# Second attention of a two-layer block: keys and values projected as four row groups of 32, and a new order of a step

## The reference, cut to what matters

```python
def _L1_xattn_ref(x, cond, w_q, w_k, w_v, w_out, b_out):     # x layer-normed, cond = ctx_768
    q = (x @ w_q).reshape(B, SQ, 16, 64)
    k = (cond @ w_k).reshape(B, SKV, 16, 64)                  # 96 -> 1024
    v = (cond @ w_v).reshape(B, SKV, 16, 64)                  # 96 -> 1024
    attn = softmax(einsum('bqhd,bkhd->bhqk', q, k) * 64 ** -0.5)
    return einsum('bhqk,bkhd->bqhd', attn, v).reshape(B, SQ, 1024) @ w_out + b_out
```

## Time and profile before

| what | value |
|---|---|
| median of three runs | 968.55 us (965.89 to 970.06) |
| time of the profiled execution | 966.52 us |
| its span, first to last instruction | 964.4 us |
| mean granted TensorE clock | 0.956 |
| TensorE busy | 881.0 us, 91% of the span |
| VectorE, ScalarE, GpSimd busy | 608.7, 557.5, 448.0 us |
| second attention, steps b = 1 to 30 | 357.98 to 781.86 us |

### The profile page before, as it was taken

How to read it: one execution, slowest core, us unless ns; L and a number is a source line. 1 busy time by engine, 2 the same in 40 slices (tenths; PEclk the granted TensorE clock), 3 DMA queues, 4 the chain that set the end, 5 groups by cost and what they waited for, 6 DMA issues and landing times.

```text
span 964.4 us, 27621 instructions
## 1 busy us (share of the span) xinstructions
PE 881.0 (91%) x10662; PEld 729.4 (76%) x10662; DVE 608.7 (63%) x1601; ACT 557.5 (58%) x1138; POOL 448.0 (46%) x544
## 2 busy tenths in 40 slices
PE   7998998778899879999999999999999998898884
PEld 3565655543799768988988888888898887878883
DVE  5887776751122377778788897878887656434442
ACT  3787676531566556666666666666666642335551
POOL 7124333357000266556656655655654343544453
PEclk7998898968999989999999999999999999999998
DMA  5345321211444233730000000000000000234330
GB/s 143 103 115 143 101 94 53 71 34 44 127 132 135 73 132 123 231 120 15 16 12 18 14 12 17 15 13 16 14 12 6 4 2 34 73 115 111 97 93 7
DMA packets 69761, 64.94 MB, mean 67 GB/s; under 512 B 13153, under 2 KB 61608, under 8 KB 68866
## 3 DMA queue, kind: packets, MB, share of 16 engines
q1 hardware_dynamic: 61698, 48.23, 16.9%
q0 software_dynamic: 7136, 14.71, 4.9%
q10 hardware_dynamic: 800, 0.24, 0.1%
HBM read 32.99 MB, written 28.39 MB: 64 GB/s over the span
## 4 chain that ended last, share of the span: by engine, by line
PE 65%; issue 15%; DVE 10%; POOL 3%; ACT 3%; DMA 2%; another core or an unknown queue 1%; SPq 1%; ACTq 0%; DVEq 0%; POOLq 0%
PE sf L964 7%; PE sf L977 6%; PE of L1013 6%; PE sf L956 5%; PE sf L1237 5%; PE jf L948 4%; PE sf L1203 4%; PE sf L1193 3%; PE jf L964 3%; PE sf L800 2%; PE sf L952 2%; PE mf L827 1%; PE sf L1106 1%; PE of L846 1%; DVE oh L1747 1%
## 5 line engine op out<-in xcount | busy, mean ns | idle before, releaser
L667 POOL TENSOR_TENSOR pl<-pT,ph 128x512 bf16<-128x512 f32 x128 | 146.0, 1163 | 118.4 <-DVE ph L1676 117.8
L656 POOL DMA_INDIRECT gb<-eo,slots x64 | 65.5, 1023 | 103.3 <-DMA eo<-rows 88.5
L1529 DVE TENSOR_REDUCE cmx<-mf 128x8 bf16<-128x1024 f32 x64 | 78.3, 1224 | 42.6 <-PE mf L827 30.2
L617 POOL DMA_INDIRECT buf<-gu,slots x64 | 63.0, 985 | 89.5 <-PE of L846 73.1
L1369 ACT ACTIVATE pT<-sf 128x1024 f32<-128x1024 f32 x64 | 65.5, 1024 | 49.6 <-PE sf L983 49.6
L1682 DVE TENSOR_REDUCE cmxb<-mf 128x8 bf16<-128x1024 f32 x64 | 78.1, 1221 | 5.3 <-PE mf L1000 5.3
L977 PEld LDWEIGHTS sf<-qTs,kTs 64*128 64x128 f32 x1024 | 62.1, 187 | 24.6 <-issue 22.7
L1301 ACT ACTIVATE pTf<-sf 128x1024 f32<-128x1024 f32 x64 | 62.5, 1021 | 28.4 <-PE sf L807 18.2
L977 PE MATMUL sf<-qTs,kTs 64*128 64x128 f32 x1024 | 74.3, 285 | 0.0
L964 PE MATMUL sf<-ctxT,wk 96*128 96x128 f32 x504 | 71.5, 286 | 1.7 <-issue 1.7
L745 POOL DMA_INDIRECT out<-rows x47 | 45.6, 971 | 48.9 <-DVE rows L1970 38.8
(11 more groups left out here) (272 smaller groups left out, 2638.3 us busy)
## 6 DMA issues: line engine op xcount, KB each, us to landing
buf<-zero SPq DMA_DIRECT2D x12, 516.0 KB
rows<-buf SPq DMA_DIRECT2D x47, 129.0 KB
buf<-zero SPq DMA_DIRECT2D x20, 256.0 KB, 3.8
rows<-buf SPq DMA_DIRECT2D x40, 128.0 KB, 2.2
eo<-rows SPq DMA_DIRECT2D x40, 128.0 KB, 2.1
gu<-in_gu SPq DMA_DIRECT2D x4, 1024.0 KB
rows<-in_x SPq DMA_DIRECT2D x8, 256.0 KB, 4.8
gu<-in_w SPq DMA_DIRECT2D x2, 1024.0 KB
```

Of the source, the lines that this page charges most:

```text
L617: nc.gpsimd.indirect_dma_start(out=buf0[:, :], out_offset=bass.IndirectOffsetOnAxis(ap=slots0[:, k, b:b + 1], axis=0), in_=xna0[:, b, :], ...
L656: nc.gpsimd.indirect_dma_start(out=gb[t % 4 * 2 + k][:, :], out_offset=None, in_=eo0[:, :], in_offset=bass.IndirectOffsetOnAxis(ap=slots0[ ...
L667: nc.gpsimd.tensor_tensor(pl[h][:, :, c, :], pT[h][:, :, c, :], ph[h][:, :, c, :], ALU.subtract)\
L1529: nc.vector.reduce_max(to, mf[:, :, :].rearrange("p c (j k) -> p c j k", j=QH), AX.X)\
```

## The change

The context is laid out as three blocks (CB = 3) of 32 rows, and each block is stored four times over the 128 partitions. The weights of keys and values are stored with the 256 output columns of a row group in its 32 partitions. `keys(n)` makes all keys of a batch with 24 matmuls of 32 rows x 128 columns, `values_of(n)` all values with 12 of 32 rows x 256 columns; the four row groups write to four banks. The fills "k" and "v" are gone, the banks of the others are fixed, and the order of a step changes on all engines. The rest of the diff merges semaphores (`selector_set`, `odds_done`), moves one memset and adds the packed arrays on the host.

```diff
-        ctxT = [sb(f"ctxT{p}", [DC, P]) for p in range(2)]
+        ctxT = [sb(f"ctxT{p}", [P, CB, P]) for p in range(2)]
+def bank_for(name, n, b):
+    if b >= LAST:
+        return {"oT0": 0, "oT1": 2, "y": 0}[name]
+    if (name, n) == ("q0", 2):
+        return 2
+    return {"q0": 0, "q1": 2, "oT0": 1, "oT1": 2, "y": 2}[name]
@@ tensor engine
+                def keys(n):
+                    banks = [mf[:, 0, :], mf[:, 1, :]] + ([of, jf] if n < 2 else [sf[:, 2, :], sf[:, 3, :]])
+                    pe.wait_ge(L1.ctx_in[n % 2], 16 * (n // 2 + 1))
+                    if n < 2:
+                        need(pe, L1.k_free, 2 * n)
+                    else:
+                        pe.wait_ge(L1.v_free, 2 * n - 1)
+                        pe.wait_ge(L1.moved_done, MOVED1[n - 2] + 1)
...
+                    for c in range(2):
+                        for u in range(CB):
+                            for i in range(QH):
+                                rr = slice(32 * i, 32 * i + 32)
+                                last = nc.tensor.matmul(banks[i][:, c * P:(c + 1) * P], wk1[rr, u, c * P:(c + 1) * P],
+                                                        ctxT[n % 2][rr, u, :], start=(u == 0), stop=(u == CB - 1))
+                def values_of(n):
...
+                        pe.wait_ge(L1.exp_done, 2 * n)
+                        L1.free(pe, "oT0", n - 2)
...
+                    for u in range(CB):
+                        for i in range(QH):
+                            rr = slice(32 * i, 32 * i + 32)
+                            last = nc.tensor.matmul(sf[:, i, 0:UC], ctxT[n % 2][rr, u, :], wv1[rr, u, :],
+                                                    start=(u == 0), stop=(u == CB - 1))
@@ score_half
+                    pe.wait_ge(L1.k_free, 2 * b + 1 + h)
+                    if h == 0:
+                        pe.wait_ge(L1.v_free, 2 * max(b, 1) + 2)
@@ tensor engine, attention: prologue keys(0), values_of(0), keys(1), values_of(1), and the step
                         score_half(b, 0)
-                        coarse_half(b + 1, 0)
                         fill("q1", b + 1)
                         weigh(b - 1, 2)
-                        fill("k1", b + 1)
+                        coarse_half(b + 1, 0)
+                        if inside(b + 2):
+                            fill("q0", b + 2)
                         weigh(b - 1, 3)
                         score_half(b, 1)
                         coarse_half(b + 1, 1)
                         fill("oT0", b - 1)
                         fill("oT1", b - 1)
+                        weigh(b, 0)
+                        values_of(b + 1)
+                        turn(b)
+                        fill("y", b - 1)
                         if inside(b + 2):
-                            fill("q0", b + 2)
-                        weigh(b, 0)
-                        if inside(b + 2):
-                            fill("k0", b + 2)
-                        fill("y", b - 1)
-                        turn(b)
-                        fill("v0", b + 1)
+                            keys(b + 2)
                         weigh(b, 1)
-                        fill("v1", b + 1)
@@ ScalarE, step: exp 0, q1, q0, exp 1, oT0, oT1, take_values, turn, take_keys (two copies of mf, two of sf 2 and 3)
+                    for to in (kTb, kT):
+                        last = nc.scalar.copy(to[p][:, 0:4, :].rearrange(n2, b=2), mf[:, :, 0:UC])
+                    last.then_inc(L1.k_free, 1)
@@ VectorE, step
-                        half_max(b + 1, 0)
+                        if inside(b + 3):
+                            normal_before(b + 3)
                         evacuate(b - 1, 2)
                         high_half(b, 0)
+                        half_max(b + 1, 0)
+                        evacuate(b - 1, 3)
                         if inside(b + 4):
                             stats_before(b + 4)
-                        if inside(b + 3):
-                            normal_before(b + 3)
-                        evacuate(b - 1, 3)
-                        if inside(b + 4):
                             aggregate_before(b + 4)
                         half_max(b + 1, 1)
                         high_half(b, 1)
                         if inside(b - 2):
                             normal_after(b - 2)
-                        if b % QH == 3 and 0 <= (b - 7) // QH:
-                            choose_expert((b - 7) // QH)
                         evacuate(b, 0)
                         if ranked_at(b - 1) is not None:
                             keep_ranks(ranked_at(b - 1))
+                        low_values(b + 1)
                         add_output(b - 1)
                         stats_after(b - 1)
                         evacuate(b, 1)
                         aggregate_after(b - 1)
-                        low_values(b + 1, 0)
-                        low_values(b + 1, 1)
+                        if b % QH == 3 and 0 <= (b - 7) // QH:
+                            choose_expert((b - 7) // QH)
```

More of the change, by code:

```diff
@@ L943, in fill @@
                     need(pe, L1.pj_free[bk], use)
+                    if name == "q0" and n == 0:
+                        pe.wait_ge(L1.v_free, 4)
+                    if name == "q1" and n == 0:
+                        pe.wait_ge(L1.k_free, 4)
+                    if name == "q0" and n >= 3:
+                        pe.wait_ge(L1.k_free, 2 * (n - 1) + 2)
+                    if name == "oT0" and inside(n + 2):
+                        pe.wait_ge(L1.k_free, 2 * (n + 2) + 2)
                     if name == "y":
@@ L953, in fill @@
                                                        o1[p][:, 8 * h + 2 * c:8 * h + 2 * c + 2, :], ident[:, :])
-                    elif what == "v":
-                        pe.wait_ge(L1.ctx_in[p], 16 * (n // 2 + 1))
-                        last = nc.tensor.matmul(ps, ctxT[p][:, :], wv1[:, 512 * h:512 * (h + 1)], start=True, stop=True)
-                    else:
-                        if what == "q":
-                            pe.wait_ge(L1.moved_done, MOVED1[XMOVE[n]] + 1)
-                        else:
-                            pe.wait_ge(L1.ctx_in[p], 16 * (n // 2 + 1))
-                        w, rhs = (wq1, xrn[p][:, 0, :]) if what == "q" else (wk1, ctxT[p][:, :])
+                    else:
+                        pe.wait_ge(L1.moved_done, MOVED1[XMOVE[n]] + 1)
@@ new lines, in values_of @@
+                def values_of(n):
+                    pe.wait_ge(L1.ctx_in[n % 2], 16 * (n // 2 + 1))
+                    if n < 2:
+                        need(pe, L1.v_free, 2 * n)
+                    else:
+                        pe.wait_ge(L1.exp_done, 2 * n)
+                        L1.free(pe, "oT0", n - 2)
+                        if inside(n + 1):
+                            L1.free(pe, "q0", n + 1)
+                    for u in range(CB):
[3 more added lines that the diff above has]
+                                                    start=(u == 0), stop=(u == CB - 1))
+                    last.then_inc(L1.v_full, 1)
@@ L1046, in attention @@
                 def attention():
-                    for name, n in step_fills(-2):
-                        fill(name, n)
+                    keys(0)
+                    values_of(0)
+                    keys(1)
+                    values_of(1)
                     turn(-2)
-                    for name, n in step_fills(-1):
-                        fill(name, n)
+                    fill("q0", 0)
+                    fill("q1", 0)
                     coarse_half(0, 0)
@@ L1390, in attention @@
                 def attention():
-                    for b in range(-2, 0):
-                        for name, n in step_fills(b):
-                            take(name, n)
-                        turn(b)
+                    take_keys(0)
+                    take_values(0)
+                    take_keys(1)
+                    take_values(1)
+                    turn(-2)
+                    take("q0", 0)
+                    take("q1", 0)
+                    turn(-1)
                     exponential(0, 0)
@@ L1405, in attention @@
                         take("q1", b + 1)
-                        take("k1", b + 1)
+                        if inside(b + 2):
+                            take("q0", b + 2)
                         exponential(b, 1)
```

125 lines of the change are left out of this document (70 added, 55 removed).

## The result

The changed kernel takes 987.37 us, median of 4 runs (979.73 to 991.32); the kernel before, on the same chip, 968.27 (965.89 to 970.06, 4 runs). The ratio is 1.0189, with a 95% interval of 1.0123 to 1.0256: slower, by between 1.2 and 2.6%, and 2.4 us above the high end of my range. The profiled execution took 986.17 us, its span is 984.4, against 966.52 and 964.4.

The account below looks back on a forecast made before the run. It took the tensor engine's stream as the bound: -6.1 + 0.7 - 1.5 + 0.9 + 3.6 + 1.1 = -1.3 us, 966.5 to 965.2 profiled; median forecast 967.5, range 958 to 985.

Parts of the forecast that it names:

- The step of four row groups: Tensor engine, each step: keys take 1.65 us and values 1.63, with four row groups side by side every 0.11 us.
- Rival A: Keys: four groups do not load fp32 weights side by side at 128 columns; +43 us, 1010; chance 0.06.
- Changes of mode: Tensor engine: switching between 128 rows and row groups costs 0.09 us in, 0.10 out, 0.10 for the next fp32 unit.
- Rival D: Tensor engine: leaving a mode behind fp32 costs the whole tail, 0.07 us more per exit; 972 to 980; chance 0.10.
- The length of a step: Second attention: a step near 13.86 us, 0.26 saved less a 0.05 wait for "oT0"; 0.21 times 29 makes -6.1.
- Ranks: VectorE: if keep_ranks' last operation is held until L667 ends, keys wait 0.9 us, six times; +3.6 taken, between 0 and 5.4.
- rival B: VectorE: low_values itself is held by GpSimd's L667, so keys wait 0.9 us every step; +22, 990; chance 0.12.
- So only two things count: Whole kernel: only the length of the tensor engine's stream and whether the new order makes it wait matter.
- Prologue and step 0: Prologue +1.1 us, between 0 and 2.5, for longer keys and more copies; step 0 +0.7 for all keys of batch 2.
- the bound that I gave the clock: Prologue: the 3.4 us stretch at the 1.2 GHz level can vanish or double, 1.7 us either way.
- `choose_expert`: VectorE every fourth step: moved to the step's end, the tensor engine sees 0.15 us of it, six times; +0.9.
- Step 30: Last step: loses "k1" and 0.24 us of values, pays 0.19 for the coarse half, fills a 0.47 wait; -1.5.

Follow-up runs that it names:

- run 4: Changed kernel with its order and banks, but keys and values contracted over 96 rows and the old 48 KB context tile; 987.41 us, ratio 1.018.
- run 3: Changed kernel with coarse_half(b + 1, 0) put back behind score_half(b, 0) on the tensor engine; 980.87 us, ratio 1.0131.
- run 11: The changed kernel unedited, timed again on another chip; 933.72 us, ratio 1.0074 to the kernel before.
- run 7: Changed kernel with 96-row matmuls, plus the four-fold context load of 192 KB into a tile nobody reads; 936.29 us, a single run.
- run 2: Changed kernel with the later loads of expert weights and zeros in smaller parts over more steps (EPARTS 16); 978.47 us, ratio 1.011.
- run 10: Changed kernel with low_values ahead of keep_ranks, coarse half back beside the scores, expert weights in eight parts, zeros spread; 919.25 us, ratio 0.993.
- run 1: Changed kernel with VectorE's low_values ahead of keep_ranks; 976.35 us, ratio 1.0062.
- run 9: Changed kernel with low_values ahead of keep_ranks and the coarse half back beside the scores, later loads left alone; 924.41 us, ratio 0.9993.
- run 5: Changed kernel with low_values ahead of keep_ranks, later loads in sixteen parts, coarse half back beside the scores; 919.63 us, ratio 0.9937.
- run 6: Changed kernel with low_values first, sixteen-part loads, coarse half back, and the prologue's key copies shared by ScalarE and VectorE; 918.85 us, ratio 0.9935.
- run 8: The kernel before with the later loads in smaller parts; 929.09 us, ratio 1.0039.

## Why the prediction was wrong, point by point

**The step of four row groups: right.** Of keys, the next weigh comes 1.55 after their start (512.30 to 513.85), and with the way in of 0.09 that is 1.64 of the predicted 1.65. Values take 1.51 to `turn`, with the way in 1.60 of 1.63. Rival A is refuted: fours stand 0.11 apart.

**Changes of mode: right.** The last record of keys starts at 513.65 and the next weigh at 513.85; less a slot of 0.11 that is 0.09, so leaving fp32 costs no tail. Rival D, and with it the reading of the Trainium skill, "TensorEngine Tiling (Array Packing)", Key Properties, as a drain of 0.17, is refuted.

**The length of a step: 14.04 for 13.86,** so the 29 x 0.21 of the sum did not come; an ordinary step saves 0.03. Two terms were short. Values wait for "oT0" from 508.11 to 508.39, 0.28 behind the last weigh, where 0.03 + 0.09 belong to the stream: 0.16 instead of 0.05. And y takes 1.97 to keys (510.33 to 512.30), of which 0.09 are the change of mode: 0.10 more than the 1.78 of the earlier trace rows. In the new order `turn` stands ahead of it, and behind the router's small matmuls its first weight load seems uncovered; I had charged such a lead-in to keys and "q0", not to y. (Run 4, with no change of mode behind y, has 1.87.) The units themselves are 0.04 shorter than reckoned. By runs 3 and 4 the split is: the row groups -0.41, the coarse half +0.21, the remaining order and its waits +0.17; together the measured -0.03.

**Ranks: the step of the sum that said "if its last operation is held".** It gave 0.9 in each of six steps and was shaded to 3.6; the runs show 8.6 in one profile and 4.6 in another. Only five can stall, and in the profile of the result the first operation was held, not the last: 1.72 above an ordinary step (15.76 to 14.04) in each, 8.6. Run 11 shows the reckoned case: 14.96, 0.92 in each, 4.6. The row of before gave a mean of 1.80, which I read as "held in all six cases". Five were held, for 2.10 to 2.15, and the sixth, in step 29, took 0.22. I took it that a start ahead of L677 would save the operation. L666, which stands ahead of L677, was not reckoned with. The Trainium skill, "SBUF — State Buffer", two separate sides, gave the right kinds: the tensor_tensor with two SBUF inputs took 3.00, and the one that reads PSUM, `low_values`, took 0.69 beside L677:

```profile
L1762 DVE TENSOR_TENSOR va10l<-sf,va10h 128x512 bf16<-128x512 f32 x28 | 18.1, 688 | 13.9 <-ACT va10h L1429 13.8
...
L1827 DVE TENSOR_TENSOR wk<-rkq,oh 128x64 f32<-128x64 f32 x5 | 15.0, 2991 | 0.0
...
L1790 DVE TENSOR_SCALAR xn<-rows,mvA,rsA 128x128 f32<-128x128 f32 x27 | 9.2, 341 | 0.1
```

So rival B is refuted, though its 990 lies near the result. L1790 fell from 1168 ns (L1717 before, the mean of 27) to 341, below the 0.41 I had named.

**The program's length: the step that failed most.** The prediction said "So only two things count": how long the tensor engine's stream becomes, and whether the new order makes it wait. A third, the loading of the program, it put at nothing, without a reason. "Hidden" was said of the context load, rightly (run 7). But the change adds 16% to the matmul records of the tensor engine, and their instructions come through the DMA engines too, in steps where these are full. That costs 7.9 us in steps 3 and 4, 4.9 as standstills and the rest behind them, together more than all the gains that I forecast. Runs 2, 7 and 10 take away the burst or the longer program, each with the same end: no stall in steps 3 and 4; runs 1, 3, 9 and 11 keep both and stall. With the later loads in sixteen parts, short ones remain in step 5 of runs 5 and 6 (0.6 and 0.3). The queue of instructions shows 1.65 MB in 101 packets for the changed kernel, some 16 KB each. The Trainium skill, "Runtime: NRT & Kernel Launch", Instruction fetch mechanics, says that an engine's sequencer fetches its program in blocks of 16 KiB over a DMA queue of its own, which agrees with the packets, and that the cost of crossing from one block to the next is mostly hidden, which the stalls here don't bear out. That the instructions come late is inferred: from the fixed places of the stalls in the program, two packets apart, and from the packet that ends 0.9 to 1.6 us ahead of the end of each. Why a program an eighth shorter has no such stall under the same burst (run 7) isn't shown any further.

**Prologue and step 0: +1.1 + 0.7 forecast, +5.1 in the first profile.** The granted clock there, after and before:

```profile
335.00:340.00 5.00, 4.20 (x36) 0.50 0.19 57
340.00:345.00 5.00, 3.50 (x16) 0.50 0.89 288
345.00:350.00 5.00, 2.27 (x28) 0.84 0.95 341
350.00:355.00 5.00, 5.00 (x36) 0.50 0.10 29
```

```profile
335.00:340.00 5.00, 3.24 (x27) 1.00 0.73 220
340.00:345.00 5.00, 2.90 (x37) 0.89 0.93 311
345.00:350.00 5.00, 4.68 (x55) 0.77 0.37 125
350.00:355.00 5.00, 2.46 (x36) 0.91 0.05 15
```

15 us at or near the 1.2 GHz level instead of a few, behind an idle stretch of the tensor engine. Nine profiles of the new order with row groups give 31.80 to 36.20, mean 34.0; two of the old order 29.94 (before) and 33.99 (run 8). The +5.1 compares one of the slower with the fastest there is. A difference of 2, near the forecast 1.8, fits them, and so does none (run 4 and run 7, in the new order with 96 rows, have 35.94 and 35.92): this stays open, and the bound that I gave the clock, 1.7 either way, was too small; the spread is 4.4.

**`choose_expert`: the term was half an account, and right in its half by luck.** The step behind the new place takes 14.30 to 14.33, of which 14.04 are an ordinary step and 0.13 the ranks' own matmuls in `turn`, as before (14.20 to 14.07). That leaves the predicted 0.15, but it isn't `choose_expert`: in run 11, the same kernel, these steps mostly take 14.17, and VectorE is as early in both (in step 12 its last operation ahead of `low_values` starts 8.96 us into the step). In the first profile keys wait for ScalarE's copy behind `turn`, late as in run 3 (the first copy of the values starts 10.33 us into step 12, in run 11 9.63). In the old place `choose_expert` had cost 0.48 to 0.60 in five steps (14.55 to 14.67 for 14.07; the sixth, 27, nothing), and that is gone; L1820, held there for 2156 ns as L1747, takes 225. The five pairs of steps come to -1.8, where I had +0.9.

**Step 30:** -1.1 for -1.5. **Between chips** the same kernel was 1.9% and 0.7% slower than the one before, which no bound of mine held: of the 11.3 us between the two differences of medians, 6.3 are in steps 1 to 30 (437.31 and 431.04), and 4.0 of these in the ranks.

**The sum** missed the +20.0 of the spans by 21.3: the step's gain 5.2, ranks 5.0, instructions 7.9, prologue and step 0 3.3 (perhaps by chance), step 30 0.4, the stretches ahead and behind 1.4, steps 5 and 6 0.6 (0.5 of it a standstill of the same kind), less 2.7 of `choose_expert`; that leaves 0.2 in rounding.

## What to carry to other kernels

Splitting matmuls into more, smaller row groups pays for its changes of mode only if few are needed, and it lengthens the engine's program: count the added instructions and look where the DMA engines are full, since code comes through them as well, and spread those loads first. When an operation that reads only SBUF on VectorE is moved, set its new time against every instruction of GpSimd, indirect DMAs too, and put what the critical engine waits for ahead of it. A change that loses can hold a gain: with two calls swapped, one unit back in its place and thinner loads, this one is 0.6 to 0.7% faster than the kernel before (runs 5 and 10).

## What was not expected of the hardware

Four fp32 row groups of 32 rows load weights and multiply 128 columns at 0.11 us for all four, as fast as one group of 128. With the DMA engines at 0.92 to 1.00 and 298 to 339 GB/s in windows of 5 us the tensor engine stood still for 1.3 to 3.6 us without a semaphore, with 12326 matmul records in its program and not with 10790, at the same few records of the program in each run and until 0.9 to 1.6 us after a 16 KB packet of instructions. And one short operation of VectorE that starts 0.30 us behind an indirect DMA of GpSimd takes 0.21 us; 0.33 behind it, it is held until the tensor_tensor after the DMA ends, and takes 3.0.
